# A layer of feed-forward, attention and feed-forward on one core: where the second-last batch's output and feed-forward products are placed in the last batch's slots

## The chip, the core and the metric

The kernel runs on one core of a Trainium2 chip. The core has the matrix engine TensorE (PE), the engines VectorE (DVE), ScalarE (ACT) and GpSimd (POOL), and the queue of SyncE (SP), which here issues all DMAs. The metric is the device time of one execution in microseconds (us); lower is better.

## The reference

The input x has the shape 4 x 1024 x 512 in float32. Each of the four batches is independent:

```
def ffn(x):                 # weight: 512 x 512, made ternary
    scale = mean(abs(weight))
    w_t = clip(round(weight / (scale + 1e-10)), -1, 1)
    return x @ (w_t * scale).T + bias

def attn(x):                # 16 heads of 32
    q, k, v = split(x @ Wqkv + bqkv)       # thirds
    scores[s, t] = k[s] . q[t] / sqrt(32)  # per head
    scores = triu(scores) - 10000 * tril(ones, -1)
    attn = softmax(scores, over s)         # a query t sees keys s <= t
    return (attn.T @ v) @ Wo + bo

x = x + 0.5 * ffn(layernorm(x))
x = x + attn(layernorm(x))
x = x + 0.5 * ffn(layernorm(x))
```

The matrix products of the projections and of the scores are made with float32 operands split into a high and a low part and three products of the parts.

## The kernel before

A batch has 8 tiles of 128 rows and 4 groups of 4 heads. The work of a batch on its row tiles is cut into units, each named by a letter and the tile:

- T1, F1: transposition of the normalised tile and the first feed-forward product; T2: transposition for the attention; V: values product.
- O: output product of the attention (12 matmuls of 512 columns); T3, F2: transposition of the normalised tile (4 transposes) and the last feed-forward product (8 matmuls of 512 columns). After F2 the tile is stored to the output.

The attention of a group runs over 10 steps (STEPS = 10: 3 for the first half of the 1024 query columns, 7 for the second), so a batch has 40 steps. Its other units are P (query and key products, 12 matmuls), A (a block of scores whose row maxima and sums are taken: PE, then DVE's maximum, then ACT's exponential with a running sum), M and N (transpositions of maxima and of reciprocals, which SP then spreads by small DMAs into `mneg` and `rall`) and C (a product that spreads the reciprocals, by which the finished chunk is scaled).

The order of the work is written out by hand in tables of rows. One row is one slot, and a slot of a batch holds one attention step. A row has up to four parts, separated by `|`: units, A blocks, tile loads, weights. P, A, M, N, C are taken from running lists, so that a letter only says "the next one"; O, T3, F2 and X3 carry the tile number. `plan()` (L268 on) turns the rows into SLOTS, and each engine then runs through SLOTS in its own order. For O, T3, F2 and X3 the batch is `ended`: the batch before, and in LAST_ROWS and TAIL_ROWS the last batch itself. In all batches but the first, GROUP0_ROWS, GROUP1_ROWS and the first slot of GROUP2_ROWS hold O, T3 and F2 of the preceding batch; GROUP2_ROWS and GROUP3_ROWS hold T1, F1, T2, V of the next batch, which in the last batch don't exist. So in the last batch slots 0 to 20 hold O, T3 and F2 of the third batch, slots 21 and 22 only P, slots 23 to 30 no product at all, and from slot 34 on come O, T3 and F2 of the last batch. "Slot n" below is slot n of the last batch where no other batch is named.

In a slot PE does: the scores of the step (12 or 24 matmuls at L1162 and 4 or 8 at L1170, which need `mneg`), the values product of the step before (L1190), the A block (L1128), then the small units (M L1138, N L1143, C L1147, T3 L1083), then the large ones (O and P at L1066, F2 at L1091). ACT does: four exponentials of the scores (`prob`, L1000), the last head of the A block of the slot before (`masked_scores`, L972), the high-part copies of M and N and the evacuation for C (L962), the copy of a T3 (L938), the high part of the attention output for an O of the next slot (L993), the first three heads of its A block, and the copies of P (L924). DVE takes maxima (L817), low parts (L792, L794), normalises the tile of the next slot's T3 (L786), adds residuals (O L803, F2 L806) and takes statistics. POOL masks the exponentials on the diagonal (L719), adds biases (L685) and makes the low part for an O of the next slot (L692).

PE's results go into a ring of seven PSUM banks, taken in program order: scores and A take four each, every other unit one. A bank is written again only when its last holder has been read. The split tiles `hts` are two, taken in the order of F1, F2 and O units; the chunks `o` are ten. The tiles `xt` are seven, taken in the order of the loads.

SP's program in a slot: store of T2's tile; store of the F2 tiles of the slot before (it waits for DVE's residual sum); the slot's loads; the small DMAs of M and N; the next weights for P. Each waits its turn behind the ones before it.

Slot starts in the trace (first matmul of the scores, us): slot 0 877.55, slot 8 925.15, slot 13 957.68, slot 18 987.74, slot 20 1000.79, slot 23 1020.12, slot 24 1023.09, slot 30 1051.52, slot 31 1056.75.

Of the kernel before, what the change touches and what calls it, by code (L numbers as in the profile page):

```python
# [12 lines left out]
P = 128  # L13
B, S, D = 4, 1024, 512
# [12 lines left out]
HI, LO = 0, 1  # L27
# [9 lines left out]
STEPS = sum(CHUNK_STEPS)  # L37
# [4 lines left out]
VG = GROUPS - 1  # L42
# [27 lines left out]
def maxima(b, g, c):  # L70

    return [("A", b, g, c, kc, tiles) for kc, tiles in QUERIES[c]]


def pieces(b, g):
    second = (Q_, K_) if g == 0 else (K_, Q_)
    return [("P", b, g, K_, 0), ("P", b, g, Q_, 0)] + [("P", b, g, j, 1) for j in second]
# [8 lines left out]
GROUP0_ROWS = (  # L86
    "C P | A | LO",
    "N M P | A | X3.0",
    "P | A | X3.1",
    "C O.0 | A | X3.2",  # L90
    "O.1 | A | X3.3",
    "N T3.0 O.2 | A",
    "M F2.0 | A | X3.4",
    "T3.1 O.3 | A",
# [3 lines left out]
GROUP1_ROWS = (  # L98
    "C T3.3 P | A | X3.6",
    "N M F2.3 P | A | X3.7",  # L100
    "P | A",
    "C O.4 | A",
    "O.5 | A",
    "N T3.4 O.6 | A",
    "M F2.4 | A",
    "T3.5 O.7 | A | X1.0",
# [3 lines left out]
GROUP2_ROWS = (  # L110
    "C T1.0 F2.7 P | A | X1.3",
    "N M T1.1 F1.0 P | A | X1.4",
    "T1.2 F1.1 P | A | X1.5",
    "C T1.3 F1.2 | A | X1.6",
    "T2.0 T1.4 F1.3 | A",
    "N T2.1 T1.5 F1.4 | A | X1.7",
    "M T1.6 F1.5 | A",
    "T2.2 T1.7 F1.6 | A",
# [15 lines left out]
FIRST_ROWS = (  # L134
    "P P | A",
    "N M P | A | | W",
    "P | A | | W",
    "C V.4 | A | | W",
    "V.5 | A | | W",
    "N V.6 | A | | W",  # L140
    "M V.7 | A | | W",
    " | A",
    " | A",
    "P | A",
)
LAST_ROWS = (
    "C | A",
    "N M | | X3.0",
    " | | X3.1",
    "C | | X3.2",  # L150
# [59 lines left out]
def plan():  # L210

    nxt = {
        "P": iter([u for b in range(B) for g in range(GROUPS) for u in pieces(b, g)]),
        "A": iter([u for b in range(B) for g in range(GROUPS) for c in range(CHUNKS) for u in maxima(b, g, c)]),
        **{kind: iter([(kind, b, g, c) for b in range(B) for g in range(GROUPS) for c in range(CHUNKS)])
           for kind in ("M", "N", "C")},
        "W": iter([("W", n) for n in range(len(WEIGHTS))]),
    }

    def words(text, b, ended):  # L220
        out = []
        for word in text.split():
            if word in nxt:
                u = next(nxt[word], None)
                if u is not None:
                    out.append(u)
                continue
            kind, *at = word.split(".")
            of = ended if kind in ("O", "T3", "F2", "X3") else b + 1
            if kind == "B":  # L230
                out.append(("B", 0))
                continue
            if kind in ("LV", "LO"):
                of = b
                if b < 1 or (kind == "LV" and b == B - 1):
                    continue
            if 0 <= of < B:
                out.append((kind, of, *[int(a) for a in at]))
        return out

    def rows(text, b, ended):
        parts = (text.split("|") + ["", "", ""])[:4]
        return [words(part, b, ended) for part in parts]

    slots = [Slot(-1, None, q, rows(text, -1, -1)) for q, text in enumerate(HEAD_ROWS)]
    for b in range(B):
        first = FIRST_ROWS if b == 0 else GROUP0_ROWS
        last = LAST_ROWS if b == B - 1 else GROUP3_ROWS
        for n, text in enumerate(first + GROUP1_ROWS + GROUP2_ROWS + last):
            ended = b if last is LAST_ROWS and n >= STEPS * VG else b - 1  # L250
            own = b - 1 if first is FIRST_ROWS and n < STEPS else b
            slots.append(Slot(b, n, None, rows(text, own, ended)))
    slots += [Slot(B, None, q, rows(text, B, B - 1)) for q, text in enumerate(TAIL_ROWS)]
    return slots


SLOTS = plan()
USES = [u for s in SLOTS for u in s.uses()]
assert len(USES) == len(set(USES))
# [972 lines left out]
```

How the kernel before makes its waits and increments, by code:

```python
            def load_x(w):  # L527
                kind, b, t = w
                if XAT[w] >= NX:
                    sp.wait_ge(x_out[XAT[w] % NX], 16 * (XAT[w] // NX))
                if kind == "X3":
                    sp.wait_ge(*stored(("X1", b, t)))
                sp.dma_start(x_tile(w), (x if kind == "X1" else xscr)[b, P * t:P * t + P, :])\
                    .then_inc(x_in[XAT[w] % NX], 16)
# [1 line left out]
            def load_raw(n):  # L536
                w = WEIGHTS[n]
                if n >= RAW:
                    sp.wait_ge(w_split, n - RAW + 1)
                to = raw(n).rearrange("p (k n) -> p k n", k=KC) if w[0] == "QK" else raw(n)
                sp.dma_start(to, source(w)).then_inc(w_raw[n % RAW], 16)
# [15 lines left out]
            def keep(n):  # L557
                sp.wait_ge(w_split, n + 1)
                sp.dma_start(wscr[n], home(WEIGHTS[n]).bitcast(F32)).then_inc(w_kept[n], 16)
# [1 line left out]
            def load_qk(u):  # L562
                _, b, g, j, _ = u
                if (b, g) == (B - 1, GROUPS - 1):
                    return
                n = WAT["QK", (g + 1) % GROUPS, j]
                sp.wait_ge(w_kept[n], 16)
                sp.wait_ge(ring_full, full(u))
                sp.dma_start(wqk[:, j, :, :, :].rearrange("p l k n -> p l (k n)").bitcast(F32), wscr[n])\
                    .then_inc(wqk_in[j], 16)
# [1 line left out]
            def rows(u):  # L573
                _, b, g, c = u
                sp.wait_ge(ring_free, freed(u))
                for part in (HI, LO):
```

## Time and profile before

| | us |
|---|---|
| median of 3 runs (lowest, highest) | 1144.65 (1144.04, 1145.78) |
| the profiled execution | 1141.25 |
| its span, first to last instruction | 1139.5 |

| engine | busy us | share of the span |
|---|---|---|
| PE | 1080.3 | 95% |
| PE weight loads | 699.9 | 61% |
| DVE | 742.8 | 65% |
| ACT | 920.6 | 81% |
| POOL | 343.4 | 30% |

The mean granted clock of PE is 0.973 of full speed. Matmuls are pipelined and their ends are modelled, so that PE's busy time also contains waits between overlapping matmuls. In the chain that ended last, PE has 75% of the span, ACT 10%, DVE 9%. The averages hold stages with different limits; the stage that matters here is the last batch, from 877.55 us to the end.

### The profile page before, as it was taken

To read this page: it belongs to the slowest core of one execution; us is meant where nothing else is said; L and a number is where in the kernel's file an instruction comes from. 1 tells how busy PE (TensorE), PEld (TensorE's weight loads), DVE (VectorE), ACT (ScalarE), POOL (GpSimd) and SP (SyncE) were. 2 spreads that over 40 slices of the span, in tenths; PEclk is the share of its full clock that TensorE was granted. 3 is DMA by queue.
4 is the path that set the end of the run, shared out by engine and by line. 5 is a ranking of instruction groups with operands and counts; after the bars stand their busy time and mean duration, and the time that the engine had idled before them with its cause. 6 is when DMAs were issued, how large, how long until landed. Compare 5 with 4: busy or idle time off the path is not lost.

```text
span 1139.5 us, 26100 instructions
## 1 busy us (share of the span) xinstructions
PE 1080.3 (95%) x9466; PEld 699.9 (61%) x9466; DVE 742.8 (65%) x2304; ACT 920.6 (81%) x2571; POOL 343.4 (30%) x471
## 2 busy tenths in 40 slices
PE   3688999999999999999999999999999999999896
PEld 3465655565666666665666666675666666664465
DVE  6776545479744766779753666879853676755344
ACT  1249899778988988978998989978997989989641
POOL 4731120135401232435301332435401332400243
PEclk9898999599999999999999999999999999999899
DMA  7432311111112221321112121321112221000121
GB/s 249 156 111 76 113 58 40 48 58 40 49 39 85 68 67 49 122 93 41 48 40 85 68 67 49 122 75 51 48 49 85 68 66 49 21 21 12 31 74 37
DMA packets 41967, 77.71 MB, mean 68 GB/s; under 512 B 5488, under 2 KB 11632, under 8 KB 41840
## 3 DMA queue, kind: packets, MB, share of 16 engines
q1 hardware_dynamic: 41840, 76.04, 20.0%
q8 instruction: 76, 1.25, 0.4%
q14 instruction: 51, 0.42, 0.1%
HBM read 49.81 MB, written 25.17 MB: 66 GB/s over the span
## 4 chain that ended last, share of the span: by engine, by line
PE 75%; ACT 10%; DVE 9%; issue 2%; POOL 2%; DMA 1%; SPq 0%; DVEq 0%; ACTq 0%; POOLq 0%
PE bank L1066 30%; PE bank L1190 10%; PE bank L1128 10%; PE bank L1162 10%; PE bank L1091 7%; ACT masked_scores L972 5%; PE bank L1083 3%; ACT prob L1000 3%; PE bank L1170 3%; DVE masked_scores L817 3%; DVE st L767 2%; DVE hn L786 1%; POOL xt L685 1%; DVE xt L806 1%; POOL rstd L675 1%
## 5 line engine op out<-in xcount | busy, mean ns | idle before, releaser
L817 DVE CUSTOM_DVE_ANT_0 masked_scores<-bank,mask 128x512 f32<-128x512 f32 (+3 forms) x768 | 380.0, 554 | 232.5 <-PE bank L1128 230.1
L972 ACT ACTIVATE masked_scores<-masked_scores,mst 128x512 f32<-128x512 f32 (+3 forms) x768 | 467.3, 618 | 5.4 <-DVE mst L817 5.4
L1000 ACT ACTIVATE prob<-bank 128x512 f32<-128x512 f32 (+1 forms) x640 | 301.9, 558 | 59.5 <-PE bank L1170 58.3
L719 POOL TENSOR_SCALAR_AFFINE_SELECT prob<-prob 128x512 f32<-128x512 f32 (+1 forms) x96 | 78.6, 818 | 391.3 <-ACT prob L1000 390.6
L1066 PE MATMUL bank<-hT,wqk 128*128 128x512 f32 x768 | 193.5, 402 | 0.0
L1162 PE MATMUL bank<-qT,kT 32*128 32x512 f32 (+2 forms) x2304 | 176.2, 381 | 3.6 <-DVE mst L817 2.6
L1128 PE MATMUL bank<-kT,qT 32*128 32x512 f32 (+2 forms) x2304 | 166.8, 382 | 8.4 <-ACT prob L1000 4.6
L1128 PEld LDWEIGHTS bank<-kT,qT 32*128 32x128 f32 x2304 | 96.8, 188 | 125.6 <-issue 62.4
L1066 PEld LDWEIGHTS bank<-hT,wqk 128*128 128x128 f32 x768 | 143.6, 192 | 37.7 <-ACT prob L1000 7.5
L972 ACT ACTIVATION_READ_ACCUMULATOR masked_scores<-masked_scores,mst 128x1 f32 x768 | 155.1, 202 | 0.0
L1162 PEld LDWEIGHTS bank<-qT,kT 32*128 32x128 f32 x2304 | 102.0, 187 | 71.2 <-issue 45.0
L1190 PE MATMUL bank<-prob,v 128*32 128x512 f32 (+3 forms) x1344 | 141.3, 508 | 0.0
L1091 PE MATMUL bank<-wfT,hts 128*128 128x512 f32 x512 | 136.5, 410 | 1.6 <-DVE hts L792 1.6
L1091 PEld LDWEIGHTS bank<-wfT,hts 128*128 128x128 f32 x512 | 94.2, 194 | 21.8 <-DVE hts L792 2.5
L685 POOL TENSOR_TENSOR xt<-xt,hb 128x512 f32<-128x512 f32 x64 | 82.2, 1284 | 71.4 <-DVE hn L786 71.4
L1066 PE MATMUL bank<-wvo,hts 128*128 128x512 f32 x384 | 98.0, 405 | 4.4 <-POOL hts L692 4.4
L1066 PE MATMUL bank<-wvo,hT 128*128 128x512 f32 x384 | 95.6, 401 | 0.0
L1066 PEld LDWEIGHTS bank<-wvo,hts 128*128 128x128 f32 x384 | 71.4, 192 | 25.0 <-ACT prob L1000 6.5
L1066 PEld LDWEIGHTS bank<-wvo,hT 128*128 128x128 f32 x384 | 71.2, 191 | 17.5 <-ACT prob L1000 1.8
L1083 PE MATMUL bank<-ident,hn 128*128 128x128 f32 x384 | 61.0, 289 | 18.9 <-DVE hn L786 18.9
L1170 PE MATMUL bank<-mneg,onesr 2*128 2x512 f32 (+2 forms) x768 | 72.0, 352 | 2.3 <-DMA mneg<-mrow 2.3
L938 ACT ACTIVATE hts<-bank 128x512 fp32r<-128x512 f32 x64 | 38.1, 596 | 38.2 <-PE bank L1083 17.9
(87 smaller groups left out, 1000.3 us busy)
## 6 DMA issues: line engine op xcount, KB each, us to landing
wqk<-weight_scratch SPq DMA_DIRECT2D x30, 512.0 KB, 3.3
wvo<-weight_scratch SPq DMA_DIRECT2D x20, 512.0 KB, 5.8
xt<-in_L_attn_x_dram SPq DMA_DIRECT2D x32, 256.0 KB, 4.4
residual_scratch<-xt SPq DMA_DIRECT2D x32, 256.0 KB, 2.0
xt<-residual_scratch SPq DMA_DIRECT2D x32, 256.0 KB, 2.9
out_dram<-xt SPq DMA_DIRECT2D x32, 256.0 KB, 2.0
o<-in_L_attn_Wqkv_dram SPq DMA_DIRECT2D x12, 256.0 KB, 4.2
weight_scratch<-o SPq DMA_DIRECT2D x6, 512.0 KB, 3.4
```

Source lines behind the costliest of these rows:

```text
L685: nc.gpsimd.tensor_tensor(to, to, (bo2 if l == 1 else hb)[:, :], ALU.add).then_inc(xb_done[l], 1)
L719: nc.gpsimd.affine_select(out=part, in_=part, compare_op=ALU.is_ge, fill=0.0, base=0, pattern=[[0, 4], [0, m], [1, P]], channel_multiplier ...
L817: nc.vector.tensor_tensor_reduce(masked_scores[:, h, at:at + n], psum(u, h)[:, at:at + n], mask[:, off:off + n], -SCALE, BIG, ALU.add, ALU ...
L972: nc.scalar.activation(of, of, ACT.Exp, bias=mst[:, c + kc, to:to + 1], scale=-1.0, accum_out=ssum[:, c + kc, to:to + 1]).then_inc(a_free, 1)
L1000: nc.scalar.activation(prob[:, at % 2, h, off:CW], psum(("S", b, n), h)[:, off:CW], ACT.Exp, scale=SCALE)\
L1066: m = nc.tensor.matmul(psum(u), left(x, k), right(y, k), start=(n == 0), stop=(n == len(terms) - 1))
L1083: m = nc.tensor.transpose(psum(u)[:, P * k:P * k + P], hn[:, TURN[u] % 2, P * k:P * k + P], ident[:, :])
L1091: m = nc.tensor.matmul(psum(u), h[:, part, k, :], wfT[:, k, :], start=(k == 0 and part == HI), stop=(k == KC - 1 and part == LO))
L1128: m = nc.tensor.matmul(psum(u, h)[:, at:at + n], query_piece(b, g, c)[row, x, P * r:P * r + P], kT[g % 2][row, y, CW * kc:CW * kc + n], st ...
L1162: nc.tensor.matmul(psum(u, h)[:, at:at + CW - off], kT[g % 2][row, x, P * kb:P * kb + P], query_piece(b, g, c)[row, y, off:CW], start=(ter ...
L1170: m = nc.tensor.matmul(psum(u, h)[:, at:at + CW - off], onesr[row, :], mneg[row, c, off:CW], start=False, stop=(kb == keys[-1]))
L1190: m = nc.tensor.matmul(accv[HD * h:HD * h + HD, off:CW], v_of(b, g, kb, h), prob[:, at % 2, h, of:of + CW - off], start=(kb == 0), stop=(k ...
```

## The change

The last batch gets row tables of its own for groups 0 to 2, and its fourth group's first slot gets an F2. O, T3, F2 and the loads X3 of the preceding batch are placed otherwise; P, A, M, N, C and LO stand where they stood. T3.2 goes from slot 8 to 11, F2.2 from 9 to 12, T3.3 from 10 to 14, F2.3 from 11 to 15, T3.4 and O.6 from 15 to 16, F2.4 from 16 to 17, T3.5 and O.7 from 17 to 18, F2.5 from 18 to 23, T3.6 from 18 to 24, F2.6 from 19 to 25, T3.7 from 19 to 28, F2.7 from 20 to 30. The loads X3.3 to X3.7 go from slots 4, 6, 8, 10, 11 to 5, 7, 10, 12, 14. `ended` becomes the last batch one slot later, so that the F2.7 in slot 30 is still the preceding batch's.

```
+LAST_GROUP0_ROWS = (
+    "C P | A | LO",
+    "N M P | A | X3.0",
+    "P | A | X3.1",
+    "C O.0 | A | X3.2",
+    "O.1 | A",
+    "N T3.0 O.2 | A | X3.3",
+    "M F2.0 | A",
+    "T3.1 O.3 | A | X3.4",
+    "F2.1 | A",
+    "P | A",
+)
+LAST_GROUP1_ROWS = (
+    "C P | A | X3.5",
+    "N M T3.2 P | A",
+    "F2.2 P | A | X3.6",
+    "C O.4 | A",
+    "T3.3 O.5 | A | X3.7",
+    "N F2.3 | A",
+    "M T3.4 O.6 | A",
+    "F2.4 | A",
+    "T3.5 O.7 | A",
+    "P | A",
+)
+LAST_GROUP2_ROWS = (
+    "C P | A",
+    "N M P | A",
+    "P | A",
+    "C F2.5 | A",
+    "T3.6 | A",
+    "N F2.6 | A",
+    "M | A",
+    " | A",
+    "T3.7 | A",
+    " | A",
+)
 LAST_ROWS = (
-    "C | A",
+    "C F2.7 | A",
     "N M | | X3.0",
...
-        first = FIRST_ROWS if b == 0 else GROUP0_ROWS
+        first = FIRST_ROWS if b == 0 else LAST_GROUP0_ROWS if b == B - 1 else GROUP0_ROWS
         last = LAST_ROWS if b == B - 1 else GROUP3_ROWS
-        for n, text in enumerate(first + GROUP1_ROWS + GROUP2_ROWS + last):
-            ended = b if last is LAST_ROWS and n >= STEPS * VG else b - 1
+        middle = LAST_GROUP1_ROWS + LAST_GROUP2_ROWS if b == B - 1 else GROUP1_ROWS + GROUP2_ROWS
+        for n, text in enumerate(first + middle + last):
+            ended = b if last is LAST_ROWS and n > STEPS * VG else b - 1
```

## Rows read from the trace of the kernel before

**Rows 1.** Chain of waits, last batch: start us, length us, what.

```profile
1020.19 0.90 PE bank L1162 x10
1021.38 0.82 ACT prob L1000 x2
...
1062.28 0.15 ACT rrow L931
...
1064.73 1.67 DMA mneg<-mrow
```

**Rows 2.** Busy time by stage: stretch, length, then each engine's busy us (instructions).

```profile
877.55:1020.12 142.57, 142.54 (x1349) 93.38 (x1349) 97.19 (x316) 128.23 (x369) 39.90 (x55) 1.00 0.16 52
1023.09:1056.75 33.66, 31.25 (x293) 16.03 (x293) 18.12 (x68) 33.66 (x97) 2.45 (x3) 0.95 0.04 10
```

**Rows 3.** Timeline of PE, slots 18, 20 and 22: start us, length us, what.

```profile
990.57 0.66 PE L1083 MATMUL bank<-ident,hn 128*128 128x128 f32 x4
990.98 2.07 PE L1091 MATMUL bank<-wfT,hts 128*128 128x512 f32 x8
992.98 0.98 PE L1162 MATMUL bank<-qT,kT 32*128 32x256 f32 x24
...
1003.85 2.11 PE L1091 MATMUL bank<-wfT,hts 128*128 128x512 f32 x8
...
1008.60 0.80 PE L1162 MATMUL bank<-qT,kT 32*128 32x384 f32 x12
...
1017.15 3.04 PE L1066 MATMUL bank<-hT,wqk 128*128 128x512 f32 x12
1020.12 0.97 PE L1162 MATMUL bank<-qT,kT 32*128 32x512 f32 x12
```

**Rows 4.** Timeline of PE, slots 23, 25, 30 and 31; gaps with what ended them.

```profile
1022.86 0.39 PE L1147 MATMUL bank<-rall,pick 8*128 8x512 f32 x1
...
1031.90 0.96 PE L1128 MATMUL bank<-kT,qT 32*128 32x512 f32 x9 [0.38 <-ACT prob L1000]
1032.79 0.28 PE L1143 MATMUL bank<-ident,rcol 128*16 128x128 f32 x1
...
1056.51 0.62 PE L1147 MATMUL bank<-rall,pick 8*128 8x512 f32 x1
...
1058.37 0.62 PE L1162 MATMUL bank<-qT,kT 32*128 32x384 f32 x8 [0.17 <-DVE mst L817]
...
1059.25 1.06 PE L1190 MATMUL bank<-prob,vx 128*32 128x512 f32 x8
```

**Rows 5.** Timeline of ACT: exponentials of slots 24, 25, 31; later two copies in a row.

```profile
1026.50 2.07 ACT L1000 ACTIVATE prob<-bank 128x512 f32<-128x512 f32 x4
...
1031.22 2.09 ACT L1000 ACTIVATE prob<-bank 128x512 f32<-128x512 f32 x4
...
1059.87 1.60 ACT L1000 ACTIVATE prob<-bank 128x384 f32<-128x384 f32 x4
...
1118.11 0.60 ACT L938 ACTIVATE hts<-bank 128x512 fp32r<-128x512 f32 x1 [6.68 <-PE bank L1066]
1118.60 0.71 ACT L993 ACTIVATE hts<-o 128x384 fp32r<-128x384 f32 x2
```

**Rows 6.** The page's issues of residual tiles, then SP's timeline from slot 26.

```profile
xt<-residual_scratch SPq DMA_DIRECT2D x32, 256.0 KB, 2.9
...
1041.70 0.38 SPq L533 DMA_DIRECT2D xt<-residual_scratch  x1
1062.76 1.34 SPq L586 DMA_DIRECT2D rall<-rrow  x2
```

**Rows 7.** Busy time by stretch, first and last batch; the column behind POOL is the granted clock.

```profile
195.00:200.00 5.00, 4.62 (x38) 2.10 (x38) 2.95 (x12) 5.00 (x13) 0.00 (x0) 1.00 0.01 3
200.00:210.00 10.00, 9.88 (x56) 4.36 (x59) 4.64 (x16) 8.13 (x23) 0.00 (x0) 0.52 0.01 2
1030.00:1035.00 5.00, 4.50 (x37) 2.13 (x37) 2.95 (x12) 5.00 (x14) 0.00 (x0) 1.00 0.01 3
```

## The prediction, made before the changed kernel was run

> **What bounds the kernel now.** I read three views in this order: the chain of waits over the last batch, the busy time by stage, and the timelines of TensorE (PE) and ScalarE (ACT) where the chain changes engine. The chain runs through PE alone up to slot 23 of the last batch, then passes to ACT at 1021.38 us and stays there until, near 1062.4 us, it goes by two small VectorE (DVE) steps and the SP queue to the DMA that brings `mneg` (landed 1066.40), on which PE waits [rows 1]. By stages: in slots 0 to 22 (142.57 us) PE is busy for 142.54 us and ACT for 128.23; in slots 24 to 30 (33.66 us) ACT is busy for all 33.66 [rows 2]. So a microsecond of PE work is worth a microsecond in the first stage and nothing in the second, as long as it fits; for ACT it is the other way round.
>
> How much fits is the question. PE's timeline in slots 24 to 30 shows matmuls drawn longer than elsewhere and gaps that ACT's exponentials or DVE's maxima end [rows 4]. A slot without products needs 2.74 us of PE for scores, values and maxima (1020.12 to 1022.86, [rows 3, 4]), while ACT's exponentials of two successive slots start 4.72 us apart (1026.50 to 1031.22, [rows 5]). That leaves 2.0 us a slot.
>
> PE's busy row for this stage says otherwise: 31.25 us of 33.66, which would leave 2.4 us in all seven slots; its weight loads are busy for 16.03 us, 48% of the stage against 65% (93.38 of 142.57) in the first [rows 2]. The Trainium skill (Perfetto Trace Analysis, Identifying the Most-Contended Engine) says that matmul busy share is no good measure of headroom, because the instructions are pipelined, and that the share of weight loads is. By the busy row the sum below would be about 1.4 us, by the weight loads the full one; I go by the slot arithmetic.
>
> **The change, part by part.** Slots 0 to 8 change only in that T3.2 leaves slot 8; the O products, the attention products and P stay in the first 23 slots. Out of these slots go F2.5, F2.6, F2.7, T3.6 and T3.7; F2.5 goes into slot 23, T3.6 24, F2.6 25, T3.7 28, F2.7 30.
>
> Removed from the stage that PE bounds: F2.5 stood alone behind a transposition and took 990.98 to 992.98, 2.00 us. F2.6 and F2.7 each stood ahead of a P; such a pair takes 4.75 us (1003.85 to 1008.60), a P alone 2.97 (1017.15 to 1020.12), so each is worth 1.78. A T3 is worth 0.41 (990.57 to 990.98). F2.3 moves from ahead of a P to a place alone and so costs 0.22 more; F2.2 moves from one P to another at no cost [rows 3]. Sum: 2.00 + 2 x 1.78 + 2 x 0.41 - 0.22 = 6.2 us. What covers this: it is a PE saving only while ACT keeps up. ACT loses two T3 copies there, so it needs about 127.2 us of the remaining 136.4, 93% [rows 2]. Where products are now lightest (slots 8, 15 and 17, one F2 each) PE needs 2.74 + 2.00 = 4.74 us and more, and ACT 4.72 plus copies of up to 0.6; but slot 6 is such a slot today between two O slots and PE shows no gap in the stage. I take nothing for it, and 0 to 2 us as its bounds, 2 being 0.7 us in each of three such slots.
>
> Added to the stage that ACT bounds:
> T3.6 and T3.7 each bring one ACT copy. Queued behind one another two ACT instructions start 0.49 us apart where the first is this copy (1118.11 to 1118.60, [rows 5]); 2 x 0.49 = 1.0 us, all on the path. Their DVE subtractions, normalisations and POOL bias sums fall beside it; DVE is busy for 18.12 of 33.66 us [rows 2].
> F2.5 in slot 23: PE needs 2.74 + 0.3 (the C row product) + 2.00 = 5.0 us up to the scores of slot 24, and the exponentials of slots 23 and 24 start 5.12 us apart (1021.38, 1026.50) [rows 1, 4, 5]. Hidden, by 0.1; without that cover it costs what is missing.
> F2.6 in slot 25: 2.74 + 0.2 (N) + 2.00 = 4.9 us against 4.72 and ACT's own small N copy: 0.1 us [rows 4, 5].
> F2.7 in slot 30: PE ends the maxima and C at 1057.13, so F2.7 ends at 1059.13. The scores of slot 31 started early and waited for DVE's maxima until 1058.37, and took 0.88 from there to the values at 1059.25; now they take at least that from 1059.13, to 1060.0 or a little later, and ACT began their exponentials at 1059.87 [rows 4, 5]. Cost 0.3 to 0.5, I take 0.4; the bounds are 0 (the low clock of this slot gone) and 2.0 (all of F2.7). Behind it on DVE's queue the residual sum of F2.7, one instruction of 128x512, now stands ahead of the reciprocal that N of slot 31 waits for, but ACT reaches its N copy only at 1062.28 and that covers it [rows 1].
>
> Queues moved past. SP's program has the store of F2.7 at the head of slot 31, so the load of the residual tile X3.0, which was issued at 1041.70, now waits for it and goes out just ahead of the small transfers for rall and mneg (1062.76 on) [rows 6]. An issue takes SP 0.4 to 0.7 us (0.38 alone, 1.34 for two), so two fit before 1062.76 if F2.7's sum ends by about 1061.4, my estimate from 1059.13 and DVE's queue; but store and load are 256 KB each and share the DMA engines with mneg, on whose landing PE waits. No row shows them together: at least 0, at most about 0.8; I take 0.3. No gain is to be had, since mneg already travels alone. Other stores and loads only change slots with time to spare: their tiles are needed slots later. POOL's splits for O.6 and O.7 move one slot, always one slot ahead of their product, as for O.3 in slot 6.
>
> Sum: 6.2 - 1.0 - 0.1 - 0.4 - 0.3 = 4.4 us off the profiled execution: its span goes from 1139.5 to about 1135.1 and its time from 1141.25 to 1136.8. The median of the timed runs, 1144.65, is 3.4 us above the profiled one; nothing of the difference touches the change, so I take it off there too: 1140.2.
>
> **Rivals.**
> A: ACT becomes the bound before slot 23, or F2.7 costs its whole length. The slot balance speaks against it, the 93% speaks for it. 4.4 - 2.0 (light slots) or 4.4 - 1.6 (F2.7): 1142.2 or 1141.8; with the DMA at its bound too 1142.7.
> B: there is no room. If PE's busy row is true, 2.4 of the 6.8 us moved fit and the rest lengthens the second stage: gain 6.2 - 4.4 - 0.4, about 1.4 us, 1143.3.
> C, slower: PE's clock. Slots 14 to 18 of the first batch have the same thin form as slots 24 to 27 here. There PE had the granted clock 1.00 up to 200 us and then 0.52, about the 1.2 GHz level, with weight loads busy 2.10 of 5 us before it; in the last batch the same share, 2.13 of 5, kept 1.00 [rows 7]. So in these rows the share did not decide. With the clock low ACT was busy for 8.13 of 10 us, 19% idle: PE had become the bound. After the change slots 26 to 29 stay thin (about 19 us). If the clock falls there, ACT's 19 us become 23.4, +4.4 us, and at half speed F2.7 takes up to 2.0 us more and the scores behind it 0.9 to 1.2, estimates by doubling their rows: 1140.2 + 7.6 = 1147.8. It decides as soon as the low stretch covers over some 60% of these slots. For it: the thin slots stay and the pieces change their place in time. Against: the last batch today goes through 30 us of thinner work at 1.00, and the change fills it. The Trainium skill (TensorE: Matmul & The Clock Gate, A second HAM failure mode: psum-queue depth-cycling) tells of a kernel whose engine idles briefly between groups while cycling through PSUM banks and whose clock then swings between its levels; by that rule the thin slots would fall to the low level as a habit and C's time would be the likely one. The first batch's trace agrees with it, the last batch's does not.
> D: more than I think: the T3 copies and F2.7 cost nothing (+1.4) and the clock that PE gets in the last 70 us falls out better by a few tenths: 1138.5.
>
> **How the numbers follow.** Forecast 0.58, A 0.14, B 0.06, C 0.10, D 0.12. Forecast 1140.2, with A's and D's sides the range is 1138.0 to 1143.6; it leaves out C and parts of B and D, under 2 in 10. A measurement of this kernel can tell about 0.2%, 2.3 us, from no change. Faster by more: forecast, D and some of A, 0.76; within: most of A and B and mild forms of C, 0.15; slower: 0.09.
>
> **What would show it.** Slot 23 starting 6.2 us earlier (1013.9) with no PE gaps before it confirms the first term; a smaller step with ACT-ended gaps in slots 8 to 18 is A. From the exponentials of slot 23 to those of slot 31, 38.5 us now, should become 40.0; 43 would be B. The mneg landing should be 4.4 us earlier; a longer flight of it is the DMA term. A granted clock near 0.5 in slots 26 to 30 is C. From the first O product on, the tail should be as long as before to about 1 us; if it is not, my prediction is wrong where I said nothing changes.

## The result, and the profile after

| | before | changed |
|---|---|---|
| median of 20 runs each (lowest, highest) | 1142.09 (1134.17, 1145.78) | 1131.78 (1129.11, 1140.89) |
| the profiled execution, time and span | 1141.25, 1139.5 | 1129.64, 1127.9 |

The ratio of the means is 0.9933 (95% interval 0.991 to 0.9956), about 7.7 us faster, where 4.4 was forecast; the medians lie 10.3 us apart, and that of the changed kernel lies below the range. Both kernels spread over some 12 us, which the three runs shown ahead of the prediction (1144.04 to 1145.78) had not let one see.

The two traces first, cut at points that both have: slot 0 and slot 23 of the last batch, the start of the exponentials of slot 31, the landing of the `mneg` rows that PE waits for (rows 1; taken where PE goes on, 0.04 us behind it), and the end.

| stretch | before | changed | difference |
|---|---|---|---|
| start to slot 0 of the last batch | 877.55 | 869.47 | -8.1 |
| slots 0 to 22 | 142.57 | 136.82 | -5.75 |
| slot 23 to the exponentials of slot 31 | 39.75 | 40.74 | +1.0 |
| from there to the landing | 6.57 | 6.60 | 0.0 |
| landing to the end | 73.1 | 74.3 | +1.2 |

The three middle rows are the change; the last one is taken up below; 8.1 of the 11.6 us lie in front of it, where the order of the work is the same in both. The changed kernel's busy time by stage (stretch, length, busy us of PE, its weight loads, DVE, ACT, POOL, granted clock, DMA) answers to rows 2 and, in its last line, to rows 7:

```profile
869.47:1006.29 136.82, 136.82 (x1316) 88.24 (x1315) 93.70 (x309) 127.20 (x367) 37.38 (x53) 1.00 0.15 49
1011.39:1045.55 34.16, 32.02 (x317) 17.29 (x317) 21.43 (x75) 34.16 (x98) 5.69 (x6) 1.00 0.05 18
200.00:210.00 10.00, 9.72 (x86) 4.79 (x86) 5.72 (x21) 10.00 (x28) 0.68 (x1) 1.00 0.12 35
```

The second line is slots 24 to 30. In the first stage PE is still busy throughout and ACT needs the 127.2 us that were reckoned; in the second ACT is still busy throughout. And in the first batch, from 200 to 210 us, the clock is 1.00 and ACT is busy for all 10 us, where rows 7 have 0.52 and 8.13. That low stretch of the kernel before lasts 27.3 us, from 200.4 us on. On the page's clock row (40 slices of 28 us, tenths of full speed) it was a 5 in the eighth slice; the changed kernel's has a 9:

```profile
PEclk9898999999999999999999999999999999999899
```

The chain of waits turns at the same places as in rows 1, with slot 23 now at 1006.29:

```profile
1006.36 0.90 PE bank L1200 x9
1007.55 0.82 ACT prob L1038 x2
...
1051.91 1.68 DMA mneg<-mrow
```

PE's timeline in slot 30, with F2.7 between C and the scores of slot 31, answers to rows 4:

```profile
1042.55 0.96 PE L1166 MATMUL bank<-kT,qT 32*128 32x512 f32 x9 [0.41 <-ACT prob L1038]
1043.12 0.40 PE L1185 MATMUL bank<-rall,pick 8*128 8x512 f32 x1
1043.50 2.11 PE L1129 MATMUL bank<-wfT,hts 128*128 128x512 f32 x8
1045.55 0.81 PE L1200 MATMUL bank<-qT,kT 32*128 32x384 f32 x12
1046.17 0.36 PE L1208 MATMUL bank<-mneg,onesr 2*128 2x384 f32 x4
1046.46 1.07 PE L1228 MATMUL bank<-prob,vx 128*32 128x512 f32 x8
```

and ACT's timeline (slots 24, 25, 30 and 31, with T3.6's copy) to rows 5:

```profile
1012.68 2.07 ACT L1038 ACTIVATE prob<-bank 128x512 f32<-128x512 f32 x4
...
1015.29 0.64 ACT L976 ACTIVATE hts<-bank 128x512 fp32r<-128x512 f32 x1
...
1017.88 2.10 ACT L1038 ACTIVATE prob<-bank 128x512 f32<-128x512 f32 x4
...
1041.93 2.00 ACT L1038 ACTIVATE prob<-bank 128x512 f32<-128x512 f32 x4
1047.03 1.57 ACT L1038 ACTIVATE prob<-bank 128x384 f32<-128x384 f32 x4
```

F2.7 ends at 1045.6, PE is through with the scores of slot 31 at about 1046.5 (1046.17 + 0.36), and ACT takes up their exponentials at 1047.03 without a gap: about 0.5 us of room. The C product takes 0.40 us at full clock, where in rows 4 it took 0.62. On SP's queue the load X3.0 went out where it was expected, and just ahead of the small transfers (rows 6), without a mark on their flight (1.68 us against 1.67):

```profile
1047.87 0.34 SPq L650 DMA_DIRECT2D out_dram<-xt  x1
1048.31 0.37 SPq L571 DMA_DIRECT2D xt<-residual_scratch  x1
1049.93 1.35 SPq L624 DMA_DIRECT2D rall<-rrow  x2
```

### The profile page after: what moved, and what is told of

It is laid out like the page before. It is cut to its first block, busy times and chain, and to the rows that moved or that the text cites. A ratio compares the mean times of both kernels' runs of the same rounds, so it can differ in the third digit from the quotient of the medians.

```text
span 1127.9 us, 26100 instructions
## 1 busy us (share of the span) xinstructions
PE 1069.5 (95%) x9466; PEld 692.7 (61%) x9466; DVE 743.3 (66%) x2304; ACT 919.7 (82%) x2571; POOL 343.4 (30%) x471
## 4 chain that ended last, share of the span: by engine, by line
PE 76%; ACT 11%; DVE 6%; issue 2%; POOL 2%; DMA 1%; SPq 0%; DVEq 0%; ACTq 0%; POOLq 0%
PE bank L1104 30%; PE bank L1228 10%; PE bank L1200 10%; PE bank L1166 10%; PE bank L1129 8%; ACT masked_scores L1010 6%; ACT prob L1038 3%; PE bank L1121 3%; PE bank L1208 3%; DVE st L805 1%; DVE masked_scores L855 1%; DVE hn L824 1%; POOL xt L723 1%; POOL rstd L713 1%; PE bank L1181 1%
## 5 line engine op out<-in xcount | busy, mean ns | idle before, releaser
L1166 PE MATMUL bank<-kT,qT 32*128 32x512 f32 (+2 forms) x2304 | 164.3, 376 | 9.5 <-ACT prob L1038 5.9
L1200 PE MATMUL bank<-qT,kT 32*128 32x512 f32 (+2 forms) x2304 | 170.5, 376 | 2.2 <-DVE mst L855 1.2
L1200 PEld LDWEIGHTS bank<-qT,kT 32*128 32x128 f32 x2304 | 98.4, 184 | 68.5 <-issue 46.2
L1228 PE MATMUL bank<-prob,v 128*32 128x512 f32 (+3 forms) x1344 | 137.4, 496 | 0.0
```

Of the source, the lines that this page charges most:

```text
L1166: m = nc.tensor.matmul(psum(u, h)[:, at:at + n], query_piece(b, g, c)[row, x, P * r:P * r + P], kT[g % 2][row, y, CW * kc:CW * kc + n], st ...
L1200: nc.tensor.matmul(psum(u, h)[:, at:at + CW - off], kT[g % 2][row, x, P * kb:P * kb + P], query_piece(b, g, c)[row, y, off:CW], start=(ter ...
L1228: m = nc.tensor.matmul(accv[HD * h:HD * h + HD, off:CW], v_of(b, g, kb, h), prob[:, at % 2, h, of:of + CW - off], start=(kb == 0), stop=(k ...
```

## The experiments

Each run lists its span and mean granted clock. From them I work out the time at low clock as 2 x (1 - clock) x span, since the low level is half of the full one: 62 us for the first trace of the kernel before, 34 for the changed one. The 20 runs of the kernel before in the first comparison have no such list and are in none of these sums; the 20 of the changed kernel are. A least-squares line of a run's time on this low-clock time and on which kernel it is gives the difference "at equal low clock"; the number behind the +- is its standard error.

### Both kernels again

No edit; a_third, a_fourth and a_fifth are the changed kernel as well.

> The kernel before once more, for the spread of its own times and for one more trace. In its first trace the granted clock was 0.5 for 27.3 us from 200.4 us on, in the first batch, where the changed kernel's trace shows 1.0; from the start of the span to slot 0 of the last batch the traces differ by 8.1 us although both kernels run the same instructions there. Theory CHANCE (the 27.3 us come and go by themselves): the times fall into two groups some 7 to 8 us apart, near 1135 and 1143, and a trace without the low stretch has slot 0 of the last batch near 869.5 us and ends near 1131.5. Rival PLACEMENT (something in the kernel before brings the low stretch every time): one group, near 1142, and the trace has it again.

> The changed kernel once more. CHANCE: two groups as well, near 1130 and 1138, in about the same proportions as the kernel before; the last batch alone, from slot 0 to the landing of mneg that slot 33 waits for, takes 184.1 us again against 188.8 in the kernel before. PLACEMENT: one group near 1130.

Measured: the kernel before 1133.07 to 1145.95 in 12 runs, median 1139.07; its trace has the low stretch again, 27.3 us from 201.7 on, with slot 0 at 878.85. The changed kernel 1132.4 to 1138.7 in 7 runs, median 1133.78. Its slot 0 lay at 868.88, and from there to the landing it took 187.5 us, not 184.2: the clock was low for 10.2 us from 1039.1 on, over slot 30. PE's timeline there:

```profile
1038.18 2.63 PE L1200 MATMUL bank<-qT,kT 32*128 32x512 f32 x12
...
1044.61 3.78 PE L1129 MATMUL bank<-wfT,hts 128*128 128x512 f32 x8
1048.32 1.25 PE L1200 MATMUL bank<-qT,kT 32*128 32x384 f32 x12
```

F2.7 takes 3.78 us there for 2.11, and the exponentials of slot 31 start 8.4 us after those of slot 30, for 5.1. These 3.3 us go straight into the stretch. The kernel before had a low stretch over its slot 30 as well and lost nothing (5.18), but it was 3.4 us long; one of 10.2 us over slots 29 and 30 cost it 1.4 us (fill_before_2 against fill_before, 191.06 and 189.61 us from slot 0 to the landing). So the changed kernel pays more for a low clock here. It is rival C in small.

The times spread as CHANCE has it, but neither trace here shows the stretch come or go within one kernel. a_fourth below does: the changed kernel has it there and not in its four other traces. The trace of only_f27_2, which runs the kernel before up to slot 20 of the last batch, doesn't have it either. So PLACEMENT is out.

### The first batch's clock held by extra work

```
 def scores(b, n):
...
+                if b == 0 and n in FILLED:      # (7, 8, 13, 14, 15, 16, 17, 18)
+                    bank_free(u, 0)
+                    for _ in range(6):
+                        nc.tensor.matmul(psum(u, 0), wfT[:, 0, 0:P], wfT[:, 0, :], start=True, stop=True)
```

> The kernel before with six matmuls of 128x512 whose results are thrown away, ahead of the scores in steps 7, 8 and 13 to 18 of the first batch (ACT bounds these slots; 1.5 us of PE more should fit into the 2.0 that are free). CHANCE: the clock stays at 1.0 there, the times lie close together near 1134 to 1136 and the two groups are gone. If the filled work doesn't hold the clock, two groups remain.

> The changed kernel with the same filling. With the first batch's clock held in both, what is left between the two is the change's own worth. CHANCE: 4 us (3.5 to 4.7, ratio 0.996 to 0.997 to the filled kernel before). Rival: the change is worth the 7.6 us that the timed runs show, the last batch having gains in runs that the two traces don't show; then the two filled kernels differ by 7 us or more.

Measured: 1139.56 (1136.99 to 1145.29, 12 runs) and 1132.47 (1132.08 to 1136.77, 6 runs); 47 and 38.5 us of low clock. Neither trace has the long low stretch; the filled kernel before at the same place and, in the last batch, in a low stretch of 3.4 us in slot 26:

```profile
200.00:210.00 10.00, 10.00 (x98) 5.46 (x90) 5.85 (x21) 10.00 (x27) 0.00 (x0) 1.00 0.01 2
1031.20:1034.60 3.40, 3.40 (x21) 1.04 (x21) 0.07 (x1) 3.27 (x8) 0.00 (x0) 0.54 0.02 5
```

None of the six traces with this filling has a long low stretch in the first batch, against six of the eleven without it, and 2 of the 66 filled runs have 57 us or more of low clock, against 104 of 185 of the two plain kernels; so the denser work held the clock there. The expected 1134 to 1136 was missed: at equal low clock the filled kernel before is 2.7 us slower than the plain one. The medians of the pair differed by 7 us, as the rival had it; 8.7 us of low clock lie between the two, worth about 2.4 us at 0.27 us each. That called for a second filling, of the last batch.

### The last batch's thin slots filled too

```
-FILLED = (7, 8, 13, 14, 15, 16, 17, 18)
+FILLED = {(0, n) for n in (7, 8, 13, 14, 15, 16, 17, 18)} | {(B - 1, n) for n in (23, 24, 25, 26, 27, 28, 29, 30)}
```

in the kernel before; (24, 26, 27, 28, 29) in the changed one.

> The filled kernel before, with the same six thrown-away matmuls also in slots 23 to 30 of the last batch. Over all runs so far time rises by 0.27 us for each us of low clock, and at equal low-clock time the changed kernel is 3.9 us faster; on top of it the filled kernel before had 47 us of low clock on average and the filled changed kernel 38. Theory EXPOSURE (the thin slots 23 to 30 of the kernel before draw low-clock stretches, and the change fills part of them): this kernel has less low clock than the filled kernel before, by 5 to 10 us (about 40), and is faster than it by 1 to 3 us although it does more work. Theory LUCK (the low-clock difference of the filled pair was chance): the same low clock, about 47, and a time from the same to 1 us longer (median 1139.5 to 1140.5).

> The filled changed kernel, with the matmuls also in slots 24 and 26 to 29 of the last batch, its thin ones. Both theories: the difference to the kernel with both fillings before is the direct part alone, 4 us (3.5 to 4.7), and the low clock is the same in both to 3 us. EXPOSURE: low clock 33 to 38, median about 1132; LUCK: 38 to 45, about 1133.

> The kernel before with the first batch's filling once more. EXPOSURE: low clock again 45 to 50 on average, median 1139 to 1140. LUCK: anywhere between 38 and 50, the mean of the two sets nearer to the changed kernel's.

> The changed kernel with the first batch's filling once more. EXPOSURE: low clock 36 to 41 again, median 1132 to 1133, 6 to 7 us below the filled kernel before. LUCK: low clock near that of the filled kernel before, and a difference of 4 us.

| kernel | runs | median | mean | mean low clock |
|---|---|---|---|---|
| first batch filled, before | 24 | 1139.3 | 1139.6 | 47.3 |
| first batch filled, changed | 18 | 1133.2 | 1133.8 | 39.0 |
| both filled, before | 12 | 1140.6 | 1140.3 | 38.7 |
| both filled, changed | 12 | 1137.3 | 1137.5 | 40.5 |

The first two rows hold both sets. With both fillings the kernel before loses 8.6 us (+-1.7) of low clock, and the difference of the pair in low clock is gone (1.8 +-2.0). So with the first batch filled, the thin slots 23 to 30 of the kernel before did draw low stretches of which the changed kernel has fewer (not none: fill_after_2 has 10.2 us in slot 30); that is EXPOSURE, and fill_before_2 repeats it (47.4 us). Not as expected: the doubly filled kernel before is not faster for it, since the extra matmuls cost 3.5 us at equal low clock; the doubly filled changed kernel, expected near 1132 with 33 to 38 us of low clock, has 1137.25 and 40.5; and the second set of the first filling has the pair 5.5 us apart (medians 1139.2 and 1133.71), between the two theories' 4 and 6 to 7. The pairs differ by 3.4 (+-0.5) and 3.2 us (+-0.4) at equal low clock.

### One step alone, one step less, one step more

F2.7 to slot 29 in the changed kernel:

```
     "T3.7 | A",
-    " | A",
+    "F2.7 | A",
 )
 LAST_ROWS = (
-    "C F2.7 | A",
+    "C | A",
```

> The changed kernel with F2.7 in slot 29 in place of slot 30. It takes apart the prediction's two terms for slot 30, 0.4 us for F2.7 and 0.3 us for the transfers behind its store. In the changed kernel's trace neither is seen: from the exponentials of slot 31 to the landing of mneg it takes as long as before. If that holds: the stretch from the exponentials of slot 23 to the landing keeps its 46.0 us within 0.2, and the time at equal low clock is the same to 0.5 us. Rival (the terms are real where the clock is low in slot 30): the stretch is 0.5 to 0.7 us shorter.

Measured: median 1138.96 (12 runs), at equal low clock 0.6 (+-0.5) slower than the changed kernel on the same chip. Its trace had the clock low for 6.8 us from 1042.7 on, over slot 29 with F2.7, so the stretch to the landing can't be compared as a whole; from the exponentials of slot 31 to the landing it took 6.61 us, as ever. It gains nothing, which speaks against both terms for slot 30. And it gives slot 30 without F2.7 at clock 1.0, which neither trace of the kernel before has: the exponentials of slots 30 and 31 start 5.11 us apart, with F2.7 between them 5.10 (the changed kernel, above).

```profile
1051.57 2.07 ACT L1038 ACTIVATE prob<-bank 128x512 f32<-128x512 f32 x4 [1.72 <-PE bank L1208]
...
1056.68 1.65 ACT L1038 ACTIVATE prob<-bank 128x384 f32<-128x384 f32 x4
```

Only F2.7 moved, in the kernel before:

```
-    "C T1.0 F2.7 P | A | X1.3",      # slot 20, in the last batch
+    "C T1.0 P | A | X1.3",
...
-    "C | A",                         # slot 30
+    "C F2.7 | A",
```

(`ended` becomes the last batch one slot later, as in the changed kernel.)

> The kernel before with one product moved: F2.7 from slot 20 to slot 30, all else as before. Slots 0 to 22 should be 1.8 us shorter than the 142.57 us (140.8), and the stretch from the exponentials of slot 23 to the landing of mneg unchanged at 45.0 us, so 1.8 us in all; with the prediction's terms for slot 30 and its queue it would be 45.7 and 1.1 us.

> Only F2.7 moved, from slot 20 to 30, once more: in the first trace the clock was low for 17.1 us from 1033.5 on, in slots 25 to 29, and the stretch from the exponentials of slot 23 to those of slot 31 took 42.9 us. With the clock at 1.0 there it should take 38.5 as in the kernel before, or 38.9 with the prediction's 0.4 for F2.7; and 6.5 or 6.8 from there to the landing of mneg.

Measured (one execution of each run): slots 0 to 22 took 140.80 us in the first trace and 140.68 in the second, as reckoned. But both traces have the clock low for 17.1 us in slots 26 to 29 (the first from 1033.5, the second from 1028.4 on), where neither trace of the plain kernel before has it. Busy time by stretch, the first trace ahead of it and in it, then the second:

```profile
1020.00:1033.00 13.00, 12.31 (x109) 5.85 (x105) 7.89 (x26) 13.00 (x33) 0.00 (x0) 1.00 0.01 1
...
1033.50:1050.60 17.10, 16.61 (x113) 7.14 (x108) 5.93 (x21) 13.45 (x35) 1.35 (x2) 0.50 0.01 3
...
1028.70:1045.80 17.10, 16.33 (x109) 7.14 (x108) 5.96 (x23) 13.23 (x36) 1.35 (x2) 0.51 0.01 3
```

ACT loses 3.7 and 3.9 us in it, and from the exponentials of slot 23 to those of slot 31 both took 42.9 us for 38.5. The gain of 1.8 us turned into a loss: from slot 0 to the landing they took 191.6 and 191.4 us for 188.9 in the kernel before. The times, 1147.62 and 1142.58 us, also hold what the first batch did: the first trace has its long low stretch, the second doesn't. This is rival C at full size, in a smaller change than the one studied. The clock was back at 1.0 by slot 30, and there the exponentials of slots 30 and 31 start 5.10 us apart with F2.7 between them, as in f27_at29 without it: F2.7 costs nothing.

One more pair moved, in the changed kernel:

```
-    "M T3.4 O.6 | A",      # slot 16
-    "F2.4 | A",
-    "T3.5 O.7 | A",
+    "M O.6 | A",
+    "T3.4 O.7 | A",
+    "T3.5 | A",
...
-    "C F2.5 | A",          # slot 23
-    "T3.6 | A",
-    "N F2.6 | A",
-    "M | A",
-    " | A",
-    "T3.7 | A",
+    "C F2.4 | A",
+    "T3.6 F2.5 | A",
+    "N T3.7 | A",
+    "M F2.6 | A",
+    " | A",
+    "F2.7 | A",
...
-    "C F2.7 | A",          # slot 30
+    "C | A",
```

(X3.7 is loaded one slot earlier.)

> The changed kernel with one more pair moved out of slots 0 to 22: F2.4 in slot 23, F2.5 and T3.6 in 24, T3.7 in 25, F2.6 in 26, F2.7 in 28; O.6 in 16, O.7 and T3.4 in 17, T3.5 in 18, so that slot 18 has no product. By the arithmetic that now holds, slots 0 to 22 lose 2.0 us more (134.8) if ACT lets them, 1.0 (135.8) if slot 18 is set by ACT; the stretch from slot 23 to the landing stays at 46 us. So 1 to 2 us faster than the changed kernel at equal low clock. Rival (ACT is the bound already, at 93% of the first stage): no gain, and PE shows gaps that ACT ends in slots 15 to 20.

Measured: median 1138.74 (12 runs), 0.8 (+-0.7) below the changed kernel on the same chip at equal low clock. In the trace slots 0 to 22 take 136.57 us for 136.82, although 2 us of PE work are gone. Slots 16 to 18 are 2.1 us shorter (16.0 for 18.1) and slot 19 gives back 1.8 (7.42 for 5.63); PE now stands idle there and its matmuls are drawn out, in slots 18 and 19:

```profile
989.15 0.66 PE L1121 MATMUL bank<-ident,hn 128*128 128x128 f32 x4
989.74 0.61 PE L1200 MATMUL bank<-qT,kT 32*128 32x256 f32 x3
990.53 0.97 PE L1200 MATMUL bank<-qT,kT 32*128 32x256 f32 x21 [0.18 <-DVE mst L855]
...
993.50 0.79 PE L1166 MATMUL bank<-kT,qT 32*128 32x384 f32 x9 [0.61 <-ACT prob L1038]
```

The rival had it right: this slot of the first stage without a product is set by ACT. From slot 0 to the landing it took 184.14 us, the changed kernel 184.16.

### The changed kernel's share of runs with a low first batch

> The changed kernel beside the three others on the same chip, for their comparison and one more trace. At equal low clock 4 us below the kernel before (3.5 to 4.6); stage 0 to 22 136.8 us again, from the exponentials of slot 23 to the landing 46.0 us where the clock is 1.0, whatever the first batch does.

> The changed kernel again, for its share of runs with the first batch's long low stretch. Runs with 57 us or more of low clock are 63 in 100 for the kernel before and 13 in 39 for the changed one, but 17 in 24 for its two variants, which run the same first batch. Within either kind of run the changed kernel is faster by 3.8 and 4.3 us. LUCK for the first batch (the same chance in both kernels): of the runs of this one and the next together 45 to 75% are of that kind, and the mean difference to the kernel before goes from 6.1 down towards 4 to 5 us. Rival (the changed kernel has it more rarely): 20 to 40%, and the difference stays above 6.

> As the run ahead of it: the second half of the same count, with one more trace of the changed kernel. LUCK: 45 to 75% of both together have 57 us or more of low clock; rival: 20 to 40%.

Measured: medians 1135.44, 1137.73 and 1137.01, 12 runs each. From slot 0 to the landing the three traces have 184.25, 184.22 and 184.20 us; a_fourth has the long low stretch in the first batch (27.3 us from 199.9 on, slot 0 at 877.2) and the two others don't (874.7 and 872.0). In a_fourth and a_fifth 13 of 24 runs had 57 us or more of low clock. LUCK was expected to give 45 to 75% and gave 54%. The cut at 57 us is a stand-in for the stretch itself: of the eleven traces without filling ten have the stretch where they have 57 us or more and don't where they have less, and the eleventh (only_f27_2, 61.6 us) has its other 17.1 us instead. All runs of all sets (one run of the kernel before with 401 us of low clock and 1201 us is left out):

| | before | changed |
|---|---|---|
| runs with under 57 us of low clock: number, mean | 44, 1135.7 | 37, 1132.5 |
| runs with 57 us or more: number, mean | 78, 1143.1 | 26, 1139.6 |
| all: number, mean | 122, 1140.4 | 63, 1135.5 |

Within a kind of run the changed kernel is 3.2 and 3.5 us faster (+-0.5 each), at equal low clock 3.3 (+-0.2). Without the changed kernel's runs of the first comparison, whose partners are not in the table, it is 3.0 (+-0.2); on the chip of a_third 3.2 (+-0.4), where 3.5 to 4.6 was expected, and on that of the last set 2.2 (+-0.3). Within a kind the low-clock times are also the same (43.5 and 42.9 us, 69.2 and 69.5), so the EXPOSURE of the filled kernels is not seen in the plain ones: what differs there is the number of runs of either kind. A microsecond of low clock costs 0.27 us. In the last set alone, 24 runs against 22, the whole difference is 3.1 (+-1.3), and over all runs it is 5.0 (+-0.6).

## Why the prediction was wrong

**The level and the spread.** The step that failed is the one that carried the sum over to the median of the timed runs: "nothing of the difference touches the change, so I take it off there too", which took 4.4 us off the median of three runs, and the range built on it. The term for the clock outside the last batch stood at nothing in both. That level was not the kernel's: a long low stretch in the first batch, which rows 7 show, was in the profiled execution and is not in every execution. Of 122 runs of the kernel before 78 had so much low clock, of 63 of the changed one 26, and of its two variants, with the same first batch, 17 of 24. In the first comparison the changed kernel had them in 7 of 20, so that its median, 1131.78, is one of a run without the stretch; the median of the kernel before, 1142.09, is in the range of its runs with it. Of the 7.7 us between the means 3.0 to 3.3 are there at equal low clock, and the rest I put down to how often the stretch came, though the clocks of those 20 runs of the kernel before are not listed. Rows 7 were read for the last batch only, and the range held no term for it; its whole size, 7 to 8 us, is larger than the change. What is left of the changed kernel's advantage, 3.0 to 3.3 us, is under the forecast of 4.4, and near the 3.5 that the two first traces give from slot 0 on (188.89 - 184.16 - 1.2). Up to the landing it is 4.7 us (188.89 - 184.16), near 4.4 by luck: the first term was 0.45 too large, and 0.7 of cost in slot 30 didn't come.

Whether the changed kernel's smaller share of such runs is chance is not settled. The order of work is the same up to slot 3 of the last batch, the last set has 13 in 24 beside 15 in 22, too few runs to tell apart, and the two variants have more of them; against it stands 26 in 63 beside 78 in 122 (19 in 43 without the first comparison). What makes the stretch come in one execution and not in the next stays open.

**The first term, 6.2 us.** It came out as 5.75, with no gap of PE. The products left as priced. What was too small is the cost of the T3 units in their new slots: T3.2 in slot 11 stands ahead of a P, and that slot took 6.60 us where 5.90 + 0.41 were reckoned; slot 16 with T3.4 took 6.69 where 6.21 (more_moved, the slot without the T3) + 0.41 come out. That is 0.37 of the 0.45 us. PE's timeline of slot 11:

```profile
936.48 0.27 PE L1176 MATMUL bank<-ident,mcol 128*16 128x128 f32 x1
936.59 0.60 PE L1121 MATMUL bank<-ident,hn 128*128 128x128 f32 x4
937.18 3.02 PE L1104 MATMUL bank<-hT,wqk 128*128 128x512 f32 x12
```

From the T3 to the product it is 0.59 us here and 0.41 in rows 3. What PE waits for in these 0.2 us no row names.

**ACT keeps up.** Right, and by little: ACT needed 127.20 of 136.82 us, and in more_moved one more pair taken out brought nothing up to the landing.

**Two T3 copies, 1.0 us.** Right: the exponentials of slots 24 and 25 start 5.20 us apart (4.72 before), those of slots 28 and 29 5.30 (4.81), 0.97 together. F2.5 hidden: right (5.13 for 5.12). F2.6 0.1: 0.07.

**F2.7 0.4 and the transfers 0.3.** Both came out as nothing at full clock. The 0.4 was reckoned from PE's end of slot 30 at low clock (rows 4); at 1.0 PE reaches F2.7 sooner after the exponentials and leaves about 0.5 us of room. Under a low stretch of 10.2 us slot 30 with F2.7 costs far more, 3.3 us (a_again; fill_after_2 has the same 187.5 us to the landing); no run shows how often that comes. For the transfers, only the issue's order was a ground; the two big DMAs were issued 3 us ahead of `mneg` and left its flight at 1.68, and from the exponentials of slot 31 to the landing it took 6.6 us in all 17 traces.

**The tail**, said to be as long as before: from the landing to the end it took 73.9 to 74.4 us in seven traces of the changed kernel, with and without filling, and 76.8 in an eighth (a_fourth); the kernel before has 73.1 in three and 76.5 to 76.8 in two filled ones. So it is 0.8 to 1.2 us longer where it is short, and as long to 0.3 us where it is long. In the first pair this goes with the low stretch behind the landing: 10.2 us from 1053.3 on cover 3.4 us of the first O product (4.56 us long), where before 6.8 us covered 1.4 of it (3.64). I had given it nothing. Whether the change brings the low stretch there or it falls so by itself no run shows.

**The rivals.** A and B did not come: in slots 0 to 22 PE has no gaps, and the stretch to the exponentials of slot 31 grew by 1.0. The busy row of PE (31.25 of 33.66 in rows 2) was a bad measure of room, as the Trainium skill (Perfetto Trace Analysis, Identifying the Most-Contended Engine) has it: 4.8 us of products and transpositions went into slots 24 to 30 (F2.5 lies in slot 23, ahead of them), and it rose to 32.02 of 34.16, while the weight loads rose from 16.03 to 17.29. C did not come in the first trace and was no fancy: it came whole in only_f27, twice, at the price given to it (4.4 us), and in part, over slot 30, in two of eight traces of the changed kernel with and without filling. In these slots of the kernel before PE's small gaps (0.38 us in rows 4, up to 0.74) end when ACT or DVE frees a bank, not with a DMA. The Trainium skill (TensorE: Matmul & The Clock Gate, A second HAM failure mode: psum-queue depth-cycling) tells of such short idling between groups of matmuls and of a clock that swings with it; here the clock fell in some executions and placements and not in others, so the case agrees in part, and that the gaps are the cause is not shown. D, the rival on the faster side, had its 0.4 us for F2.7 right and its 1.0 us for the T3 copies wrong, and it looked for the clock in the last 70 us, not in the first batch; it is not what made the time 1131.78.

## What to carry to other kernels

Look in the trace for every stretch at low clock, wherever it lies, before you take a median as the level: ask whether each execution has it, and put its whole price into the range. Compare kernels at equal low-clock time when mean clock and span are known for each run. Where PE bounds one stage and ACT the next, move only PE work across, slot by slot up to ACT's pace; here it stopped paying where an emptied slot reached that pace too.

## What was not expected of the hardware

Two executions of the same instructions differ by 7 to 8 us through one stretch of 27.3 us at a granted clock of 0.5, and a microsecond of low clock costs 0.27 us on average in this kernel. A small change of placement (one product of 2 us moved by ten slots) had the clock fall for 17.1 us in both its traces in slots where the kernel before kept 1.0 in both of its own; two traces against two don't rule out chance, and which of the slots' properties decides it was not found. The same extra matmuls that kept the long low stretch away cost 2.7 us themselves, so nothing was won by them.
